# Other distances modulo 256 bytes between weights and moving operand in a single-core graph-attention kernel

## What is computed

```python
hi_t = einsum('bid,de->bie', h, W1_w[:HID]) + dep_emb(adj) @ W1_w[HID:] + W1_b
hj_t = einsum('bjd,de->bje', h, W2_w[:HID]) + dep_emb(adj) @ W2_w[HID:] + W2_b
relevance = sum(hi_t * hj_t, axis=-1)
A = softmax(where(adj, relevance, -1e9), axis=2)
h_syn = relu(einsum('bij,bjd->bid', A, h) @ gcn_w + gcn_b)
out = layernorm(h + h_syn @ Wo_w + Wo_b)
```

## Time and profile before

| | |
|---|---|
| median of the executions timed | 378.48 us |
| span of the profiled execution, first to last instruction | 377.4 us |
| median less span | 1.1 us |
| TensorE busy | 369.0 us, 98% |
| VectorE busy | 245.0 us, 65% |
| ScalarE busy | 198.5 us, 53% |
| GpSimd busy | 145.0 us, 38% |
| mean granted TensorE clock | 0.997 |

### The profile page before, as it was taken

How to read it: one execution, slowest core, us unless ns; L and a number is a source line. 1 busy time by engine, 2 the same in 40 slices (tenths; PEclk the granted TensorE clock), 3 DMA queues, 4 the chain that set the end, 5 groups by cost and what they waited for, 6 DMA issues and landing times.

```text
span 377.4 us, 9989 instructions
## 1 busy us (share of the span) xinstructions
PE 369.0 (98%) x3859; PEld 320.1 (85%) x3859; DVE 245.0 (65%) x693; ACT 198.5 (53%) x437; POOL 145.0 (38%) x108
## 2 busy tenths in 40 slices
PE   8998999999999999999999999999999999999994
PEld 5786898988989898898989889898988989888893
DVE  1556568485765847577584757748475774847756
ACT  1576837356283735718264471826447282635562
POOL 1504552617053271705417160441716144141814
PEclk9999999999999999999999999999999999999998
DMA  7994206465342645525254552625545262550033
GB/s 226 344 328 131 77 6 214 131 180 173 91 173 83 201 146 173 174 80 185 83 187 161 171 163 76 202 83 181 167 146 169 79 217 83 168 168 3 2 126 128
DMA packets 43268, 55.48 MB, mean 147 GB/s; under 512 B 10352, under 2 KB 37488, under 8 KB 43248
## 3 DMA queue, kind: packets, MB, share of 16 engines
q1 hardware_dynamic: 42448, 54.30, 45.4%
q10 hardware_dynamic: 800, 0.90, 0.7%
HBM read 42.61 MB, written 12.58 MB: 146 GB/s over the span
## 4 chain that ended last, share of the span: by engine, by line
PE 94%; ACT 2%; DMA 2%; DVE 1%; issue 0%; POOL 0%
PE banks L462 26%; PE banks L464 25%; PE banks L463 25%; PE banks L529 7%; PE banks L483 6%; PE banks L569 2%; DMA xt_sb<-in_x_t_dram 2%; PE banks L558 1%; PE banks L510 1%; ACT less_sb L798 1%; DVE z_lo L952 1%; ACT xt_hi L795 0%; ACT prob L773 0%; PE banks L579 0%; DVE rel L970 0%
## 5 line engine op out<-in xcount | busy, mean ns | idle before, releaser
L871 DVE TENSOR_TENSOR y_sb<-banks,y_sb 128x384 f32<-128x384 f32 x60 | 33.4, 557 | 77.3 <-PE banks L464 77.3
L1144 POOL TENSOR_TENSOR y_sb<-y_sb,wob_sb 128x1536 f32<-128x1536 f32 x15 | 52.9, 3527 | 62.5 <-DVE y_sb L893 49.4
L785 ACT CAST z_hi<-banks 128x512 fp32r<-128x512 f32 x48 | 26.6, 589 | 83.2 <-PE banks L529 77.9
L462 PE MATMUL banks<-wo_hi,hs_hi 128*128 128x384 f32 x180 | 60.5, 336 | 0.0
L463 PE MATMUL banks<-wo_lo,hs_hi 128*128 128x384 f32 x180 | 60.5, 336 | 0.0
L464 PE MATMUL banks<-wo_hi,hs_lo 128*128 128x384 f32 x180 | 60.5, 336 | 0.0
L462 PE MATMUL banks<-xt_hi,m_hi 128*128 128x512 f32 x144 | 58.4, 406 | 0.0
L462 PE MATMUL banks<-z_hi,gcn_hi 128*128 128x512 f32 x144 | 58.0, 402 | 0.0
L464 PE MATMUL banks<-z_hi,gcn_lo 128*128 128x512 f32 x144 | 56.6, 393 | 0.0
L464 PE MATMUL banks<-xt_hi,m_lo 128*128 128x512 f32 x144 | 56.5, 392 | 0.0
L463 PE MATMUL banks<-z_lo,gcn_hi 128*128 128x512 f32 x144 | 56.3, 391 | 0.0
(11 more groups left out here) (108 smaller groups left out, 616.4 us busy)
## 6 DMA issues: line engine op xcount, KB each, us to landing
x_sb<-in_x_dram SPq DMA_DIRECT2D x16, 768.0 KB, 4.6
xt_sb<-in_x_t_dram SPq DMA_DIRECT2D x15, 768.0 KB, 6.6
y_sb<-in_x_dram SPq DMA_DIRECT2D x15, 768.0 KB, 4.6
out_dram<-y_sb SPq DMA_DIRECT2D x30, 384.0 KB, 2.5
adj_sb<-in_adj_dram SPq DMA_DIRECT2D x32, 64.0 KB, 3.1
xt_sb<-in_x_t_dram SPq DMA_DIRECT2D x2, 384.0 KB, 6.8
xt_sb<-in_x_dram SPq DMA_DIRECT2D x1, 768.0 KB, 6.1
w2t_sb<-in_w_t_dram SPq DMA_DIRECT2D x3, 192.0 KB, 4.6
```

Source lines behind the costliest of these rows:

```text
L462: pe.matmul(acc, a_hi, b_hi, start=first, stop=False)
L785: act.copy(by_graph(z_hi[:, f, :]), mixed(f)).then_inc(zhi, 1)
L871: dve.tensor_tensor(y_home(g, slot)[:, q, :], out_bank(g, q)[:, 0:HID], y_home(g, slot)[:, q, :], ALU.add).then_inc(added, 1)
L1144: pool.tensor_tensor(y_home(g, slot), y_home(g, slot), wob_sb[:].rearrange("p (o n) -> p o n", o=1).to_broadcast([P, PAIRS, HID]), ALU.add ...
```

## The change

A gap that holds no data is cut from 48 to 16 floats (192 to 64 bytes), and another of 16 floats stands ahead of `gcn_hi`. Weights less moving operand, modulo 256 bytes:

| product | weights | moving | before | after |
|---|---|---|---|---|
| projection | m | xt | 192 | 64 |
| gcn | gcn | z | 192 | 128 |
| output | hs | wo | 192 | 64 |
| output, group 14 | xt | wo | 0 | 0 |

All that is allocated behind `gcn_lo` starts 64 bytes lower than before. The instructions and their order are the same on every engine.

```diff
         z_lo = sb("z_lo", [P, C, GT], F32R)
-        sb("gap0", [P, 48])
+        sb("gap0", [P, 16])
         m_hi = sb("m_hi", [P, C, HID], F32R)
         m_lo = sb("m_lo", [P, C, HID], F32R)
         hs_hi = sb("hs_hi", [P, C, GT], F32R)
         hs_lo = sb("hs_lo", [P, C, GT], F32R)
+        sb("gap1", [P, 16])
         gcn_hi = sb("gcn_hi", [P, C, HID], F32R)
         gcn_lo = sb("gcn_lo", [P, C, HID], F32R)
```

## The result

The changed kernel takes **381.37 us** (median of 5, 381.12 to 382.21) against 378.48 us before: the ratio is 1.0073 with a 95% interval of [1.0055, 1.009]. It is slower by 2.9 us.

The account below looks back on a forecast made before the run. TensorE's start-to-start matmul intervals were taken to bound the kernel. At 0 ns change per matmul the span stayed 377.4 us, plus 1.1 us around it gave 378.5 us; the 8-in-10 range was 375.2 to 381.3 us.

Parts of the forecast that it names:

- rival D: Streams stay together: output product at 64 bytes, +2.7 us (381.2 us); or only passing at stage starts, +1.4 us; chance 0.25.
- the 5.85 that D named: Sign of a slowdown: the output product's 33 matmuls taking 5.85 us or more, instead of 5.71.
- item 5: DVE, ACT and POOL access other low address bits; cost 0, or 5 us if POOL slowed 10% without idle cover.
- item 4: Tensors allocated behind start 64 bytes lower; both reads of each small matmul keep their relative position, so cost 0.
- The 1.1 us that the sum took: Timed median 378.48 us less traced span 377.4 us, taken as time around the span and added to it.
- the nearest row: Group 14's output product, weights `xt` at distance 0: 173.3 to 173.5 ns per matmul, within 0.5 ns of distance 192.
- The bounds: All 1404 matmuls slowed by 5 ns, +7.0 us; or all excess over column time gone, -20.7 us.
- Rival B: New distances cut 2.5 ns from each wide gcn and projection matmul: 2.2 us gained, 376.3 us; chance 0.31.
- the narrow ones' excess: The 384-column output matmuls' time beyond their columns, 13.2 ns, which the wide matmuls might come down to.
- Rival C: Excess is a conflict of weight and moving reads and disappears: -20.7 us, 357.8 us; chance 0.04.

## Why the prediction was partly right

The forecast was no change, 378.5 us; what came is slower, 381.4 us, close to rival D's 381.2. The range reached to 381.3, so the median lies 0.07 us above its end, and the ratio applied to 378.48 (381.24) just inside. Its chance for slower was 0.25. That the range reached so far is luck: its upper end is D's price for the output product, and the loss came mostly from the wide products, for which D priced only a loss at the start of each stage. Nor was there a sign for it: 25 wide matmuls took 5.83 us, and the output product's 33 took 5.76, below the 5.85 that D named.

- **That TensorE's intervals are the time, and that nothing else would move: right.** The other engines only wait longer, no instruction or transfer was added, item 5's cost is 0 (3511 against 3516 ns), and item 4's is 0, since moving all tensors with distances kept did nothing. The 1.1 us that the sum took for what lies around the span mixes two executions: in every execution on record the time is 1.8 to 1.9 us above the span of the same one. The sum is not touched by that, since it starts from a median.
- **The step that failed** is "The value I take is that of the nearest row, the steady interval at the one other distance: 0 ns per matmul". The runs showed +4.5 ns for the gcn product (233.5 against 229.0), +4.2 for the projection (233.2) and +1.6 for the output product (174.8 against 173.2), where the forecast had 0. The row was read rightly: distance 0 does give 173.3 ns, and it still does. But it was one product and one distance, and the curve is not smooth: 0 and 192 are good while 224 between them is bad. A single row at another distance could not carry the value for 64 and 128, nor could 384 columns stand for 512. The bounds were sound, +7.0 us and -20.7 us; within them the eight kernels with all products at one distance lie between -0.3 and +4.9 us.
- **Rival D had the kind of effect, at the wrong product.** The runs show a steady interval that is longer at some distances. That the two streams "stay together" there was not observed. D priced it for the output product at 64 bytes, 540 x 5 ns = +2.7 us. There it is 1.6 ns (174.8 against 173.2), 540 x 1.6 = +0.9 us, and 3.4 ns only in the last group. The loss is in the wide products, +4.3 ns each: 864 x 4.3 = +3.7 us by the intervals. By the stage times of one group it is +3.1 us (0.09 x 16 + 0.12 x 14), since the first two matmuls of a gcn stage are not slower and the first two projections lie ahead of the first gcn product, in the stretch with the waits for loads.
- **Rival B** had the size of a gain right and its place wrong: at its best distance a wide matmul settles at 226.7 ns, near the 226.5 of "the narrow ones' excess", but that distance is 0, not 64 or 128, and entering takes back about half of the gain.
- **Rival C** falls as it was priced: at none of eight distances does the excess disappear, 13.2 to 21.0 ns are left. Weights of one column leave 13.3 to 18.5 too. A part that every load costs, wherever it reads, is not ruled out.
- **The Trainium skill**, in "TensorE: Matmul & The Clock Gate", the step on LDWEIGHTS, has it that a load takes no read bandwidth from the running matmul. By that the placement would be worth nothing. The runs do not agree: the mean interval of the wide products goes from 227.8 to 234.3 ns with the distance, and with all at 64 it falls by 1.4 to 2.2 ns when the loads alone read something else.

## What to carry to other kernels

In this kernel TensorE is the bound and every matmul loads its own weights. There the low address bits of the two operands moved the time by up to 1.1% (383.78 against 378.91 us), and one gap between tensors sets them. In a kernel of this kind they are worth a test. A neighbouring distance does not tell the value: good ones stand beside bad ones 32 bytes away, and they differ with the number of columns. So each product is swept on the chip. That takes one run for each distance, when all products are moved together and the intervals are read from starts. An edit to the size of a tensor ahead of an operand can change the distance unseen, so after a change of allocation the intervals are worth a look.

## What was not expected of the hardware

- A difference of 32 bytes in a tensor's start moves the interval of a 512-column float32r matmul from 227.8 to 233.0 ns, and one of 256 bytes moves nothing (229.0 and 229.0).
- The same product at the same distance has more than one steady interval (173.3 and 176.7 ns at 64 bytes by the trace, 174.6 in the changed kernel), and keeps it to the end of its 36 matmuls. What picks it was not isolated.
- A 512-column float32r matmul with its load never came below 224 ns singly, in the trace's starts, or 226.7 in a settled row. That is 13.4 ns over the 213.3 that its columns take at one a cycle and 2.4 GHz, an estimate. The 384-column one never settled below 173.3, 13.3 ns over its 160.0. None of eight distances and no load of a single column went below these.
